# Turned one-hots of the attention softmax made by VectorE from key rows that a DMA spreads over the partitions

## The reference, cut to what matters

```python
h = (x @ W).reshape(n, H, C)                       # n 6250, H 8, C 16
a_src = jnp.einsum('nhc,hc->nh', h, att_src)
a_dst = jnp.einsum('nhc,hc->nh', h, att_dst)
e = jax.nn.leaky_relu(a_src[src] + a_dst[dst], 0.2)
m = jax.ops.segment_max(e, dst, num_segments=n)
ex = jnp.exp(e - m[dst])
denom = jax.ops.segment_sum(ex, dst, num_segments=n)
out = jax.ops.segment_sum(h[src] * (ex / denom[dst])[:, :, None], dst, num_segments=n)
```

## Time and profile before

| | us |
|---|---|
| median of 3 executions | 10093.97 (10083.33 to 10097.08) |
| span of the profiled execution, first to last instruction | 9138.1 |
| what the median has beyond that span | 955.9 |
| attention loop: first and last gather (L1855) | 5676.4 to 6846.5 |
| busy in 5700 to 6900: TensorE, VectorE, ScalarE, GpSimd | 952.2, 859.7, 320.0, 801.6 |

### The profile page before, as it was taken

One profiled execution on the slowest core, in us unless ns is written; L12 is line 12 of the kernel. 1 busy time (PEld: TensorE's weight loads), 2 busy tenths in 40 slices (PEclk: granted clock), 3 DMA queues, 4 the chain that ended last, 5 costly groups with the idle time before them and its releaser, 6 DMA issues. The chain is left out here.

```text
span 9138.1 us, 79567 instructions
## 1 busy us (share of the span) xinstructions
PE 4929.6 (54%) x17328; PEld 3653.7 (40%) x17328; DVE 5774.6 (63%) x18939; ACT 852.5 (9%) x2178; POOL 6584.3 (72%) x6544
## 2 busy tenths in 40 slices
PE   0466015555555565555666665788884444454444
PEld 0355014344433343334433333555553444443333
DVE  8677028888566656666688887777776444454444
ACT  0000000000000000000233333222221000010000
POOL 5777777777677767777677774766664777747776
PEclk9765557777777777777767766555555555565555
DMA  2344011111211121111211122222221222222222
GB/s 46 70 100 109 1 18 52 52 52 52 60 53 53 53 60 53 53 53 52 58 48 48 48 49 47 52 50 50 50 49 57 53 53 53 53 65 53 53 53 62
DMA packets 397463, 489.89 MB, mean 54 GB/s; under 512 B 135634, under 2 KB 302358, under 8 KB 396726
## 3 DMA queue, kind: packets, MB, share of 16 engines
q0 software_dynamic: 208736, 381.82, 17.5%
q1 hardware_dynamic: 185226, 101.57, 3.9%
q10 hardware_dynamic: 3020, 1.36, 0.1%
HBM read 448.73 MB, written 37.86 MB: 53 GB/s over the span
## 5 line engine op out<-in xcount | busy, mean ns | idle before, releaser
L1832 POOL DMA_INDIRECT RING<-TAB,IDX x2418 | 2319.9, 959 | 807.6 <-issue 683.9
L1295 PE MATMUL PS<-RB,RING 128*128 128x256 f32 x4836 | 1743.7, 524 | 1325.4 <-DMA RING<-TAB,IDX 1285.6
L1295 PEld LDWEIGHTS PS<-RB,RING 128*128 128x128 f32 x4836 | 1217.9, 264 | 1851.0 <-issue 1191.2
L670 DVE TENSOR_TENSOR RA<-RA,PS 128x256 f32 x2418 | 995.2, 412 | 874.9 <-PE PS L1295 833.3
L670 DVE TENSOR_TENSOR RB<-RB,PS 128x128 f32 x2490 | 712.6, 286 | 1194.6 <-PE PS L1295 1173.3
L1295 PE MATMUL PS<-OH,RING 128*128 128x128 f32 x3324 | 809.2, 422 | 912.6 <-DMA RING<-TABM,IDX 409.5
L1781 POOL DMA_INDIRECT REC<-RC x800 | 962.5, 1203 | 299.4 <-issue 243.2
L656 DVE TENSOR_SCALAR RB<-IOTA,KEY,WE 128x256 f32<-128x256 f32 x2418 | 1080.1, 447 | 107.0 <-ACT RA L1618 48.2
L1295 PEld LDWEIGHTS PS<-OH,RING 128*128 128x128 f32 x3324 | 706.0, 314 | 1014.4 <-issue 820.1
L1846 POOL DMA_INDIRECT RING<-TABQ,IDX x806 | 895.1, 1111 | 277.6 <-issue 242.7
L1832 POOL DMA_INDIRECT RING<-TABN,IDX x830 | 787.0, 948 | 365.1 <-issue 252.8
(11 more groups left out here) (377 smaller groups left out, 6684.1 us busy)
## 6 DMA issues: line engine op xcount, KB each, us to landing
RING<-in_edge_attr_dram SPq DMA_DIRECT2D x830, 64.0 KB
RING<-TAB,IDX POOLq DMA_INDIRECT x2418, 2.5
RING<-TABN,IDX POOLq DMA_INDIRECT x830, 2.5
RING<-TABM,IDX POOLq DMA_INDIRECT x830, 2.5
RING<-TABQ,IDX POOLq DMA_INDIRECT x806, 2.6
REC<-RC POOLq DMA_INDIRECT x800, 2.6
TAB<-HN SPq DMA_DIRECT2D x18, 512.0 KB, 3.2
RING<-TABG,IDX POOLq DMA_INDIRECT x560, 2.6
```

Source lines behind the costliest of these rows:

```text
L670: v.tensor_tensor(sl, sl, sums_of(k, weighted), ALU.add).then_inc(s_ad, 1)
L1295: m = t_.matmul(sums_of(t, wide), GD[:, slot_, :], one_hot(t, wide), start=True, stop=True)
L1832: p.indirect_dma_start(GD[:, t % SLOTS, :], None, table, bass.IndirectOffsetOnAxis(ap=idx[:, t:t + 1], axis=0)).then_inc(s_ring[t // 4 % 1 ...
```

## The change

`OHTQ`, the transposes (L1471) and ScalarE's copies (L1705) are gone, with the semaphore between them. While the edges are being sorted, VectorE writes the keys of all tiles as rows of bf16 (`KRB`, one tile per partition) and a column `LANE` with the partition's own number; SyncE's queue puts the rows into DRAM (`KRD`). In the attention loop the queue loads the 16 key rows of a chunk, 2,048 keys, broadcast to all partitions, into one of two halves of `KROW` in `RA`. VectorE compares four tiles' keys, 512 columns, with `LANE`: that is the turned one-hot of four tiles. They go to one of four buffers, in `OHT` and `OHB`.

```diff
+            own_done(prep)
+            v.tensor_copy(KRB, KR[4]).then_inc(prep.sem, prep.one())
+            v.tensor_copy(LANE, tf[:, 0:1]).then_inc(prep.sem, prep.one("key_rows"))
...
             v.wait_ge(s_x, 32)
+            v.wait_ge(s_krd, 16)
             v.memset(RA[:, NP:NW * WN], 0.0).then_inc(misc.sem, misc.one())
...
                 if t < NL1 and t % 4 == 0:
                     v.tensor_tensor(OBR[:, t % 52:t % 52 + 4, :], IOTAB[:, 0:WD].unsqueeze(1).to_broadcast([128, 4, WD]),
                                     KEY1[:, t:t + 4].unsqueeze(2).to_broadcast([128, 4, WD]), ALU.is_equal).then_inc(s_ob, 1)
+                    if t % 16 == 0:
+                        v.wait_ge(s_krow[t // 16 % 2], 16 * (t // 32 + 1))
+                    if t >= 16:
+                        v.wait_ge(s_lk, t // 4 - 3)
+                    v.tensor_scalar(turned_quad(t // 4), KROW[:, t // 16 % 2, t % 16 * 128:t % 16 * 128 + 512], LANE, None,
+                                    ALU.is_equal).then_inc(s_oc, 1)
                 chain_part(t, 0)
...
             for t in range(NL1 + LAG1 + LATE1):
-                if t < NL1:
-                    q = t // 4
-                    if t % 4 == 0:
-                        t_.wait_ge(s_ob, q + 1)
-                        if q >= 2:
-                            t_.wait_ge(s_oc, q - 1)
-                    i = t_.transpose(PS[3 + q % 2][:, 64 * (t % 4):64 * (t % 4) + 64].bitcast(BF16), OBR[:, t % 52, :], IDENTB[:, :])
-                    if t % 4 == 3:
-                        i.then_inc(s_tp, 1)
...
-                    m = t_.matmul(o, OHTQ[:, a % 8, :], AD3[:, bass.ds(w, 1), :].rearrange("p a b -> p (a b)"),
+                    m = t_.matmul(o, turned_one_hot(a), AD3[:, bass.ds(w, 1), :].rearrange("p a b -> p (a b)"),
...
             for t in range(NL1 + LAG1 + LATE1):
-                if t < NL1 and t % 4 == 3:
-                    q = t // 4
-                    a_.wait_ge(s_tp, q + 1)
-                    if q >= 2:
-                        a_.wait_ge(s_lk, q - 1)
-                    a_.activation(OHTQ[:, 4 * (q % 2):4 * (q % 2) + 4, :],
-                                  PS[3 + q % 2][:, 0:256].bitcast(BF16).rearrange("p (a b) -> p a b", b=WD),
-                                  ACT.Copy).then_inc(s_oc, 1)
...
+            s_.wait_ge(prep.sem, prep.at["key_rows"])
+            s_.dma_start(KRD.rearrange("(b p) l -> p b l", p=128), KRB).then_inc(s_krd, 16)
...
             s_.wait_ge(pre1.sem, pre1.at["pads"])
             s_.dma_start(SC2[:, :], KFD).then_inc(s_kfl, 16)
+            s_.wait_ge(s_hw, 19)
+            for c in range(NC1):
+                if c >= 2:
+                    s_.wait_ge(s_oc, 4 * (c - 1))
+                s_.dma_start(KROW[:, c % 2, :], KRD[16 * c:16 * c + 16, :].rearrange("(a t) l -> a (t l)", a=1)
+                             .to_broadcast([128, 2048])).then_inc(s_krow[c % 2], 16)
```

More of the change, by code:

```diff
@@ L133, in program @@
         ATTD = dram("ATTD", (128, NW * WN))
+        KRD = dram("KRD", (NTB * 128, 128), BF16)
         (iW1, iW2, iW3, iEN, iRE, iGW, iSS, iNE, iED, iDA, iCO, iSE) = range(12)
@@ L177, in program @@
         s_klast, s_kfl = sem("key_ends_t"), sem("key_firsts")
-        s_ob, s_tp, s_oc, s_lk, s_ox, s_gx, s_mb, s_ab = (sem("g_onehot"), sem("g_turned"), sem("g_turned_sb"), sem("g_look"),
+        s_ob, s_oc, s_lk, s_ox, s_gx, s_mb, s_ab = (sem("g_onehot"), sem("g_turned"), sem("g_look"),
                                                           sem("g_onehot32"), sem("g_weighted"), sem("g_summed"), sem("g_added"))
@@ L182, in program @@
         s_bias = sem("bias")
+        s_krd = sem("key_rows_put")
+        s_krow = [sem(f"key_rows{i}") for i in range(2)]
         s_nr = [sem(f"normed{i}") for i in range(4)]
@@ L225, in program @@
         DI1 = HNF[:, 5 * 896:6 * 896].bitcast(I32).rearrange("p (b l) -> p b l", l=128)
+        KRB = HNF[:, 6 * 896:6 * 896 + 448].bitcast(BF16).rearrange("p (b l) -> p b l", l=128)
+        KROW = RA[:, 52 * 64:52 * 64 + 2048].bitcast(BF16).rearrange("p (a n) -> p a n", n=2048)
+        LANE = COLS[:, 11:12]
         GD = GR[:, 0:SLOTS * 128].rearrange("p (a d) -> p a d", d=128)
@@ L253, in program @@
         OHQ = OH[:, :, :].rearrange("p a b -> p (a b)").rearrange("p (a b) -> p a b", b=WD)
-        OHTQ = OHT[:, :, :].rearrange("p a b -> p (a b)").rearrange("p (a b) -> p a b", b=WD)
+        OHT2 = [o[:, :, :].rearrange("p a b -> p (a b)") for o in (OHT, OHB)]
         AC1 = RB[:, :].rearrange("p (n f) -> p n f", f=146)
@@ L345, in att_sums, with turned_quad, turned_one_hot @@
             return PS[t % 12 // 2][:, t % 2 * WN:t % 2 * WN + WN]
+        def turned_quad(q):
+            return OHT2[q // 2 % 2][:, q % 2 * 512:q % 2 * 512 + 512]
+        def turned_one_hot(t):
+            return turned_quad(t // 4)[:, t % 4 * WD:t % 4 * WD + WD]
         def gat_sums(t):
```

## The result

| | us |
|---|---|
| kernel before, median of 5 | 10093.07 (10083.33 to 10097.08) |
| changed kernel, median of 5 | 10050.50 (10036.96 to 10056.54) |
| ratio | 0.9955, 95% interval 0.9945 to 0.9966 |
| predicted | 10014, range 9985 to 10066 |

The change is faster by 43 us, by the interval 34 to 56. The forecast said 80: the sign and the range hold, the size is about half.

A forecast was written before the change was run, and what follows sets the result against it. The attention loop was taken as bound by VectorE's work plus its waits, in turns with TensorE; -0.94 and -0.59 make -1.53 us a chunk, -80 in 52 chunks, so 10093.97 - 80 = 10014, range 9985 to 10066.

The forecast's parts named there:

- the gate: In the attention loop, TensorE's transpose at each fourth tile waits for VectorE's one-hots L1085, ahead of the chain's matmul.
- the three waits: VectorE's waits at L995, L1014 and L1038 in the attention loop, together 2.07 us a chunk, forecast to go.
- L973's: VectorE's wait for a late TensorE, 1.52 us a chunk; TensorE forecast 0.94 earlier, 0.26 of wait left.
- x: VectorE's time for each new comparison, 208 in the attention loop: taken as 0.45 us, between 0.26 and 0.81.
- the sum: Attention loop per chunk: -0.94 up to L973 and -0.59 after, together -1.53 us, in 52 chunks -80 us.
- The row L1025: An existing VectorE comparison, median 471 ns, least 267, read as mostly waiting some 0.2 us; 0.08 was added for it.
- The rival of a slow comparison: VectorE's new comparison takes 0.6 to 0.81 us, giving -18 to -50 us, 10044 to 10076; chance 0.06.
- What is late next: After the change GpSimd follows closely in the attention loop: free of TensorE it needs 1072 us, leaving some 18 us.
- GpSimd becomes the bound: Rival, attention loop: each comparison holds back a gather for its whole length, 92 us, so no change, about 10088; chance 0.06.
- The chain's own waits (slower): Rival: waits at L995, L1014, L1038 are the chain's round trip; +47 to +94 us, 10141 to 10188; chance 0.08.
- Hidden parts: Key-row loads have a chunk of cover, some 20 us, without it 166 us in all; ScalarE's 208 copies count nothing.
- The base: Span 9138.1 us against the runs' median: the 955.9 us difference was carried over unchanged, giving span 9058, time 10014.

The follow-up runs named there:

- e_ahead: Kernel before with VectorE's one-hots made four tiles earlier; transposes and copies stay, no comparison added: 9030.92 us, ratio 0.9892.
- e_gate: Changed kernel with TensorE again waiting at each fourth tile for VectorE's one-hots, without transposes or copies: 9067.17 us, ratio 0.9932.
- e_noload: Changed kernel loading only the first two chunks' key rows, so later chunks compare with wrong keys: 9084.89 us, ratio 0.9949.
- e_ahead1: Kernel before with one-hots made three tiles ahead of first use: 9028.07 us, ratio 0.9891; again on the other level 9997.00 us, 0.9978.
- e_after: Changed kernel, unchanged, timed beside the kernel before on the same chip at the 9130 us level: 9099.47 us, ratio 0.9957.
- e_ahead2: Kernel before with the one-hots made two tiles ahead of their first use, no comparison added: 9108.86 us, ratio 0.9965.
- e_oneport: Changed kernel with the comparison, in its old place, also summing its result into a spare column: 9044.95 us, ratio 0.9910.

## Why the prediction was right, and where it was not

*What bounds the kernel, and the gate.* Right that the gate makes the three waits, as the edit of the gate alone shows (e_ahead). The three waits of 2.07 us a chunk went to 0.04, and L973's from 1.52 to 0.65, where 0.26 was forecast. But e_gate keeps 63 us of gain with the gate in place, so the gate is not the whole of it.

*The comparison.* x was taken as 0.45 us. It is 0.344 us long at the median and the next instruction starts 0.26 after it (6222.51 to 6222.77), which is the lower end of the forecast. By this the sum would have been -99, so the comparison's own length explains nothing of the half that is missing. The row L1025, from which I took 0.08 us of waiting, was of little use: the comparison takes 414 ns at most. The rule of the Trainium skill, "VectorE: DVE Perf Modes", section "What auto-detection actually checks", on 16-bit data, cited beside the sum, gave the 0.26 that was measured. The rival of a slow comparison has a slip: by the prediction's own sum x = 0.6 gives -62 us, not -50.

*GpSimd.* This is the step that failed, at the level of 9130. "What is late next" took its own pace as fixed, 1072 us, "the forecast leaves it some 18 us". It became 1142.5, and the last gather came 23 us earlier (6820.0 against 6842.7), where about 80 were forecast. The rival "GpSimd becomes the bound" had the mechanism and nearly the size, 92 us by the whole length of each comparison; measured are (1072 - 982) ns x 832 = 75 us. It had a chance of 0.06 and came to 1164 us for the loop; with 75 it is 1072 + 75 = 1147, near the 1142.5. What it lacked is the share of the one-hots, and that most comparisons hold nothing while one in each chunk holds a gather for over a microsecond. What spoke against it was the median of 947 ns, and that was the wrong number to look at: with one gather in four held, the median cannot move (it is 944 to 948 in all these variants, from -99 to -17 us). The maximum of 1616 in the same row was the hint; the mean, 984, was at hand.

That the time lies within the range was luck. With x between 0.26 and 0.6 the sum gives -99 to -62; a gain of 43 us is in the range only by the part that was kept for a slow comparison, and the comparison was fast.

Put together: on VectorE -99 us with x = 0.26; GpSimd, 75 us slower and before waiting 98 us more than issue for TensorE, could give back only 98 - 75 = 23 us between first and last gather. Measured there are 27.6 (1170.1 to 1142.5). Another 14.1 come from the end: the last addition starts 32.4 us after the last gather (6852.4), before 46.5 (6889.2 and 6842.7), since TensorE and VectorE keep close behind a GpSimd that is late. The first gather starts 4.9 us later (5677.5 against 5672.6). 27.6 + 14.1 - 4.9 = 36.8 us is the difference of the two profiled executions (9129.46 and 9092.66); the medians differ by 41.

*The chain's own waits (slower).* Excluded: the waits fell with the gate. *Hidden parts:* the loads of key rows are hidden (e_noload), each landing in 3.8 us at the median. ScalarE's copies were taken away in no run by themselves; e_ahead keeps them and wins 99 us.

*The base.* I carried 955.9 us over as lying outside the span. Two us do. The rest was a comparison across two levels. That the difference came out the same at both, -43 and -41 us, was luck: nothing in the prediction speaks for it.

Not settled is the level of 10000 to 10093 us, at which the result itself was measured. Each chip was met in one session, so whether the chip or the session sets the level is open too. All engines stop together there, also in passes that no variant touches; in the profiled executions at that level many waits end by something that the trace doesn't show ("remote"), and no DMA of the gathers has a landing time in the profile. The change gains 43 us there, the one-hots three tiles ahead only 22. In the changed kernel's execution there the mean gather is 1002 ns, and GpSimd waits 178 us for TensorE and for "remote", so that a held GpSimd ends the gain is not shown at this level. The profile of before at that level was not taken, so whether the change wins there by its gate, by its relief of TensorE or by chance of phase is open. Nor was a version found that is best on both: e_ahead1 and e_ahead, -98 and -99 us at 9130, are faster than the changed kernel there by more than 50 us, and on the other level e_ahead1's ratio of 0.9978 (before at 10019) stands behind the change's 0.9955 (before at 10093).

## What to carry to other kernels

Before moving work off an engine that is in a ring of waits, look for what stands at the head of its queue: here a transpose's wait could be removed without its work, by making its input four tiles earlier, and that won 99 us. When GpSimd issues gathers close to the loop's pace, read its mean and its tail, not its median, and price each added VectorE operation by what it does to them: the form that takes twice as long on VectorE won 40 us at the level of 9130. Time a variant on more than one chip and in more than one session before ranking by tens of microseconds.

## What the runs showed of the hardware

- A gather of 0.94 us took up to 2.09 us when a scan, a comparison of two inputs (0.65 us) and a one-source comparison (0.33 us) lay under it in one piece. With the form that sums its result, 0.74 us long, in the same place, the longest was 1.62.
- Held gathers end 0.82 us after a VectorE operation: in e_after 51 after the one-source comparison and 99 after the two-input one, in e_ahead2 147 after the two-input one. In e_oneport none does after the summing form, though 108 gathers pass 0.12 us after their start while it runs.
- The same one-hots in four places, one tile apart, gave mean gathers of 999, 999, 1081 and 1005 ns, and 67 us of time. That the reason is how VectorE's and GpSimd's periods fall against each other fits this and e_gate, and was not tested apart.
- A comparison of 512 bf16 values with a column took 344 ns, the two-input one of the same size 677 (e_after, medians).
- The same kernel took 9126 to 9141 us on three chips, 10093 where the change was measured, and 10019 on one more, each time within 0.3% of itself.
